# Group-norm statistics of a fused conv/scan kernel: sums and squares on ScalarE in place of block statistics on VectorE

## Chip, cores and metric

The kernel runs on one core of one Trainium2 chip. The metric is the device time of one execution in microseconds (us), lower is better; the time before is the median of three runs.

## What is computed

The input x has 16 images of 8 channels of 256 x 256, float32. Four residual blocks follow each other, and each normalises its input over four groups of two channels first (`_gn`):

```python
def _gn(v, G=4, eps=1e-05):
    g = v.reshape(B_, G, C_ // G, H_, W_)
    m = jnp.mean(g, axis=(2, 3, 4), keepdims=True)
    s = jnp.var(g, axis=(2, 3, 4), keepdims=True)
    return ((g - m) / jnp.sqrt(s + eps)).reshape(v.shape)

x = x + dilate3x3(_gn(x))                 # maximum over 3x3
x = x + mamba(_gn(x), ...)                # 4x4 pixel unshuffle: 128 channels, 4096 tokens, 256 inner rows, 32 states
x = x + conv3x3(_gn(x), L2_weight, L2_bias)
x = x + conv3x3(_gn(x), L3_weight, L3_bias)
```

The mamba block is a layer norm, an input projection with a causal convolution of 4 taps, SiLU, projections to dt, B and C, and for each of 32 states s the recurrence h = h * exp(dt * A_s) + (dt * x) * B_s over the 4096 tokens, y = sum over s of h * C_s, a gate and an output projection. A mean and a variance of each group of each image are what the change makes in another way; four such norms an image (called raw, x1, z0 and z1, after the tile that holds the input of each block).

## The kernel before

Everything is one program of five engine queues that are written by hand, with semaphores between them. A loop runs over the 16 images (b); in it stand 8 chunks of 512 tokens (c), and in each chunk the 32 states (s). One step (c, s) is called a state or slot here, (0, 14) for state 14 of chunk 0. Each engine's queue is written state by state, and all other work (the next chunk's projections, the dilation of the next image, the convolutions of the image before) is placed by tables into states of the queue: an engine does, at the end of what a state needs, what the tables put there.

In each state:
- ScalarE (ACT): `make_decay` makes exp(dt * A) of the *next* state in two halves into the PSUM ring `a_ps`, which has three places. Each half waits for the scan that last read its place. Then `keep` copies two columns (`carry`).
- VectorE (DVE): `scan` runs the recurrence for two halves of 128 rows x 512 tokens, out of `a_ps` and `u_in` into `h`; between them `make_u` multiplies `u_in` for the next state, out of `dtx` and `b_ps`. That is so in 22 of 32 states.
- GpSimd (POOL): `hc` = h * C of the state, and in the other 10 states `make_u`. `h` has three places, so VectorE can be at most some two states ahead of GpSimd. For each chunk GpSimd also multiplies one tile for the layer norm (`scale_tokens`, state 1), makes dt and dtx (states 23 to 27), and in chunks 1 to 4 adds the dilated rows (state 18).
- TensorE (PE): `b_ps` (the broadcast of B) for `make_u`, and the sum of `hc` over the states into `y_ps`.
- `gate` on VectorE at state 2 of a chunk waits until TensorE has summed the last state of the chunk before.

In certain states ScalarE also has the bursts that the argument comes back to: `silus` at state 14 of each chunk (two table loads and two activations), `split_hi` at 16, `softplus_in` at 21 and 23, `softplus_log` at 23, `centered` at 0, `token_rstd` at 2, `layer_norm` at 4, four `pad` (the normalised input of a convolution) a convolution, and `normalise_band` at state 6 of chunks 1 to 4.

The statistics before. VectorE reads each block of 512 elements once with the block statistics instruction (`partition_stats`, L1125), 8 blocks a norm: raw at (0, 9) to (0, 16), z0 at (0, 14) to (0, 21), z1 one by one after each block of the first convolution is copied out (in states 23, 29 and 3 of chunks 1 to 3), x1 at (5, 24) to (5, 30) and (6, 18). `group_local` (L1142) puts the 8 blocks together into a mean and a variance of each partition. TensorE then averages over the partitions of a group with a small matrix (L951), once for the mean (`group_mean`), and once for the variance plus the squared deviation of the partition's mean (`group_var`); ScalarE has `group_deviation` and `group_rstd` between and after. In chunk 0 VectorE waits for z to land before the first statistic of z0:

```python
if s == Z_STATS[1]:
    dve.wait_ge(z_in, (b + 1) * BANDS * 16)
last = z_stats(Z0, s - Z_STATS[1])
```

The blocks of z come by four DMAs that SyncE issues in states 9 to 12 of chunk 0, each of them behind a load of `c_sb` that waits for GpSimd's `hc` of that state or the one before.

Before the loop the norms of raw and x1 of the first image are made alone, behind their loads and with nothing beside them; behind the loop those of z0 and z1 of the last image.

## Time and profile before

| | |
|---|---|
| median of 3 runs | 14811.7 us (14810.26 to 14811.98) |
| profiled execution | 14813.43 us, its span 14811.6 us |
| TensorE busy | 12503.6 us, 84% |
| VectorE busy | 13954.9 us, 94% |
| ScalarE busy | 9028.1 us, 61% |
| GpSimd busy | 13564.0 us, 92% |
| granted TensorE clock, mean | 0.951 |
| idle time of GpSimd before `hc` | 839.6 us, of which 688.3 us ended by a scan of VectorE |

Busy time is the union of an engine's instructions. An instruction's duration overlaps that of its neighbour by some hundredths of a microsecond, so what an instruction adds to a queue without gaps is a little less than its duration. The loop over images lies between 217.27 us (the first `gate`) and 14637.67 us (the last), some 901 us an image. The stages below are cut at the start of `gate`, at state 2 of one chunk to state 2 of the next. Two engines are over 90% busy and hand each other work in every state, so a share of the span does not tell which one decides; that is read from who waits in which stretch.

How the views below read. The page and the groups by line give busy us, then (in groups) the mean ns of one, and behind the second bar the idle us just before them with what ended it. A window gives its length, then busy us and (x instructions) of TensorE, its weight loads, VectorE, ScalarE and GpSimd, the granted clock, the DMA share and GB/s. A timeline row has the start, the duration, engine, line and operation, the number merged (x), and in brackets the idle time before it.

### The profile page before, as it was taken

Reading aid. Unit: us, or ns where it says so; the run is one execution under the profiler, and the core shown is the slowest. Engines: PE = TensorE matmul, PEld = TensorE weight load, DVE = VectorE, ACT = ScalarE, POOL = GpSimd, SP = SyncE. Lnnn points to the kernel's source line nnn. Section 1 sums busy time; section 2 is a strip of 40 time slices with the busy share of each in tenths; the row PEclk is TensorE's granted clock in tenths of the full one; section 3 lists DMA queues with packets and bytes.
Section 4 is the critical chain, followed back from the end, with each engine's and each line's share of the span. In section 5 each row is a group of like instructions: output and inputs, shape, how many; then the busy total and the mean of one; then the engine's idle time right before and its main releaser. Section 6 shows DMA issues by size and latency. Waiting matters only on the chain.

```text
span 14811.6 us, 162715 instructions
## 1 busy us (share of the span) xinstructions
PE 12503.6 (84%) x27626; PEld 4938.6 (33%) x27626; DVE 13954.9 (94%) x12371; ACT 9028.1 (61%) x16239; POOL 13564.0 (92%) x6104
## 2 busy tenths in 40 slices
PE   4888878888888888888888888888888888888887
PEld 1333333333333333333333333333333333333332
DVE  5999999999999999999999999999999999999995
ACT  3666666666565666666666666665666666666663
POOL 4999999999999999999999999999999999999995
PEclk7999999999999999999999999999999999999998
DMA  3344443434434344443444434444343444434442
GB/s 92 108 121 115 115 121 108 127 111 114 121 110 128 108 115 122 114 122 109 116 121 115 120 109 123 114 115 121 110 129 107 114 123 114 122 110 115 121 114 80
DMA packets 1258543, 1701.83 MB, mean 115 GB/s; under 512 B 402220, under 2 KB 551156, under 8 KB 1257268
## 3 DMA queue, kind: packets, MB, share of 16 engines
q1 hardware_dynamic: 1257364, 1689.83, 40.7%
q14 instruction: 892, 7.31, 0.2%
q8 instruction: 287, 4.70, 0.1%
HBM read 1525.80 MB, written 124.13 MB: 111 GB/s over the span
## 4 chain that ended last, share of the span: by engine, by line
DVE 28%; PE 28%; issue 22%; POOL 14%; ACT 2%; DMA 2%; DVEq 1%; SPq 1%; POOLq 0%; ACTq 0%
PE y_ps L1026 17%; DVE h L1193 15%; POOL hc L659 10%; DVE u_in L1177 9%; PE proj_ps L980 3%; POOL u_in L636 3%; PE b_ps L1078 2%; PE side_ps L1037 2%; PE y_ps L1023 2%; DVE vmax L1156 1%; DMA z<-x_dram 1%; DVE stats L1125 1%; PE side_ps L1012 1%; DMA c_sb<-bc_dram 1%; DVEq L1191 1%
## 5 line engine op out<-in xcount | busy, mean ns | idle before, releaser
L659 POOL TENSOR_TENSOR hc<-h,c_sb 128x1024 f32<-128x1024 f32 x4096 | 9605.0, 2364 | 839.6 <-DVE h L1193 688.3
L1193 DVE TENSOR_TENSOR_SCAN h<-a_ps,carry,u_in 128x512 f32<-128x512 f32 x7168 | 8765.9, 1263 | 193.2 <-ACT a_ps L792 120.5
L792 ACT ACTIVATE a_ps<-dt,a_neg 128x512 f32<-128x512 f32 x8192 | 5602.5, 688 | 5166.5 <-DVE h L1193 5148.7
L1026 PE MATMUL y_ps<-hc,ident 128*128 128x512 f32 x16400 | 8169.3, 624 | 470.9 <-POOL hc L659 410.5
L1026 PEld LDWEIGHTS y_ps<-hc,ident 128*128 128x128 f32 x16400 | 3153.3, 198 | 4182.5 <-issue 3105.7
L1177 DVE TENSOR_TENSOR u_in<-dtx,b_ps 128x1024 f32<-128x1024 f32 x2816 | 3361.8, 1194 | 59.5 <-PE b_ps L1078 56.8
L636 POOL TENSOR_TENSOR u_in<-dtx,b_sb 128x1024 f32<-128x1024 f32 x1282 | 3033.8, 2367 | 0.1
L1078 PE MATMUL b_ps<-b_parts,select 96*128 96x512 bf16 x2816 | 1120.2, 398 | 1412.5 <-DVE u_in L1177 1410.4
L1193 DVE TENSOR_TENSOR_SCAN h<-a_ps,u_in 128x512 f32<-128x512 f32 x1024 | 1199.1, 1205 | 165.2 <-POOL hc L659 125.7
L1078 PEld LDWEIGHTS b_ps<-b_parts,select 96*128 96x128 bf16 x2816 | 281.9, 100 | 2944.9 <-DVE u_in L1177 2424.7
L980 PE MATMUL proj_ps<-u_ln,w_x 128*128 128x512 f32 x2064 | 974.2, 594 | 21.9 <-ACT xz L749 18.2
L1037 PE MATMUL side_ps<-padded,w_main 128*128 128x512 f32 x1632 | 872.1, 620 | 120.4 <-ACT raw L829 69.6
L798 ACT ACTIVATE carry<-h 128x2 f32<-128x2 f32 x3584 | 681.6, 190 | 0.0
L980 PEld LDWEIGHTS proj_ps<-u_ln,w_x 128*128 128x128 f32 x2064 | 390.9, 190 | 525.1 <-issue 489.3
L1041 PE MATMUL side_ps<-z,ident 128*128 128x512 f32 x544 | 517.4, 1040 | 0.0
L1037 PEld LDWEIGHTS side_ps<-padded,w_main 128*128 128x128 f32 x1632 | 320.8, 201 | 574.5 <-issue 414.6
L610 POOL TENSOR_TENSOR dt<-xz 128x512 f32<-128x512 f32 x258 | 329.5, 1277 | 61.6 <-ACT xz L783 61.6
L623 POOL TENSOR_TENSOR vmax<-norm,raw 128x1024 f32<-128x1024 f32 x68 | 277.0, 4074 | 94.3 <-DVE norm L1159 94.3
L1046 PE MATMUL side_ps<-edge,w_dt 49*128 49x512 f32 x544 | 333.8, 696 | 0.0
L617 POOL TENSOR_TENSOR dtx<-dt,xc 128x512 f32<-128x512 f32 x258 | 330.6, 1282 | 0.0
L801 ACT ACTIVATE padded<-z,g_shift,g_rstd 128x1024 f32<-128x1024 f32 x136 | 307.3, 2268 | 0.1
L1125 DVE BATCH_NORM_STATS2 stats<-z 128x6 f32<-128x512 f32 x272 | 180.6, 666 | 131.1 <-DMA z<-x_dram 69.0
(100 smaller groups left out, 6880.8 us busy)
## 6 DMA issues: line engine op xcount, KB each, us to landing
c_sb<-bc_dram SPq DMA_DIRECT2D x4100, 256.0 KB, 3.2
b_sb<-bc_dram SPq DMA_DIRECT2D x1284, 256.0 KB, 3.2
raw<-x SPq DMA_DIRECT2D x68, 512.0 KB
x_dram<-vmax SPq DMA_DIRECT2D x68, 512.0 KB, 4.7
z<-x_dram SPq DMA_DIRECT2D x68, 512.0 KB, 7.7
out<-raw SPq DMA_DIRECT2D x272, 128.0 KB
x_dram<-x SPq DMA_DIRECT2D x129, 256.0 KB, 3.9
x<-x_dram SPq DMA_DIRECT2D x136, 224.0 KB, 7.8
```

The costliest lines, as they stand in the source:

```text
L636: pool.tensor_tensor(u_in[:, s % U_RING], dtx[:, c % 2], b_sb[:, j % B_RING:j % B_RING + 1, :].broadcast_to([P, NH, T]), ALU.mult).then_in ...
L659: pool.tensor_tensor(hc[:, ring_at(c * S + s, HC_RING)], h[:, ring_at(c * S + s, H_RING)], c_sb[:, s // C_GROUP % C_RING, s % C_GROUP:s % ...
L792: act.activation(a_ps[:, a_slot(c * S + s, half)], dt[:, c % 2, half], ACT.Exp, scale=a_neg[:, at:at + 1]).then_inc(a_made, 1)
L798: act.activation(carry[:, :, s:s + 1], h[:, ring_at(c * S + s, H_RING), :, T - 1:T], ACT.Copy).then_inc(kept, 1)
L980: mm = pe.matmul(proj_ps[:, :], w_x[:, tap, half * P:(half + 1) * P], u_ln[:, tap:tap + T], start=(tap == 0), stop=(tap == TAPS - 1), skip ...
L1026: mm = pe.matmul(y_ps[:, half], ident[:, :], hc[:, ring_at((c * S + s) % (NC * S), HC_RING), half], start=False, stop=(s == S - 1), skip_g ...
L1037: pe.matmul(side_ps[:, :].rearrange("p (g w) -> p g w", w=W), w_main[n][:, part, :], padded[:, 1 + CB * k:1 + CB * (k + 1), part:part + W] ...
L1041: pe.matmul(side_ps[:, :].rearrange("p (g w q) -> p g w q", g=CB, q=R), ident[:, :], z[:, k * T:(k + 1) * T].rearrange("p (g q w) -> p g w ...
L1046: pe.matmul(side_ps[:, :], w_edge[n][:, :], edge[0:ER + 1, k % 2, :], start=False, stop=True, skip_group_check=True).then_inc(side_filled, 1)
L1078: pe.matmul(b_ps[:, :], select[:, k * P:(k + 1) * P], b_parts[:, c % 2, :], start=True, stop=True).then_inc(b_cast, 1)
L1177: dve.tensor_tensor(u_in[:, s % U_RING], dtx[:, c % 2], b_ps[:, :].unsqueeze(1).broadcast_to([P, NH, T]), ALU.mult).then_inc(u_made, 1)
L1193: dve.tensor_tensor_scan(h[:, r, half], a_ps[:, a_slot(c * S + s, half)], u_in[:, s % U_RING, half], start, ALU.mult, ALU.add).then_inc(h_ ...
```

## The change

VectorE loses all block statistics and `group_local`. ScalarE takes both passes:
- a first pass adds up each block: `sum_block` copies the block onto itself with the running sum of the instruction (`accum_out`) into `sums`; for z1 the sum rides on the copy out of PSUM that was there before (`copy_conv`).
- `group_mean` on TensorE takes 8 columns a norm in place of one; `group_average` on ScalarE adds the 8 columns and gives minus the group's mean.
- a second pass, `sum_squares`, reads each block again, as Square with the bias `g_mean`, with its running sum into `squares`, two blocks a state. What it writes goes into parts of `padded` or `norm` that are free then.
- `group_var` and `group_rstd` follow as before, with one more small activation and one more wait each.

The means move three states earlier (`MEAN_AT`), the variances 2 to 5 states later (`VAR_AT`), `pad` for z0 from (0, 28) to (1, 0) and for z1 from (4, 3) to (4, 5), the edge loads behind them, and block 6 of the second convolution from states 15 to 22 of chunk 6 to states 24 to 28.

```diff
-                            ((4, 0), (4, 1), (4, 2), (5, 0), (5, 1), (5, 2), (6, 0), (7, 0)))):
+                            ((4, 0), (4, 1), (4, 2), (5, 0), (5, 1), (5, 2), (6, 1), (7, 0)))):
     for k, (c, place) in enumerate(places):
         CONV_AT[n, k] = [c * S + s for s in PLACES[place]]
-MEAN_AT = {"joint": (0, 23), "z1": (3, 30), "x1": (6, 24)}
-VAR_AT = {"joint": (0, 26), "z1": (4, 1), "x1": (6, 27)}
+MEAN_AT = {"joint": (0, 20), "z1": (3, 30), "x1": (6, 21)}
+VAR_AT = {"joint": (0, 31), "z1": (4, 4), "x1": (6, 29)}
+SQUARES_AT = {"joint": [(0, s) for s in (21, 22, 24, 25, 26, 27, 28, 29)], "z1": [(3, 31), (4, 0), (4, 1), (4, 2)],
+              "x1": [(6, s) for s in (22, 24, 25, 26)]}
...
-PADDED_AT = ((0, 28), (4, 3))
-EDGES_AT = ((1, 0), (4, 8))
+PADDED_AT = ((1, 0), (4, 5))
+EDGES_AT = ((1, 5), (4, 10))
 LOAD_Z = (0, STORE_X2 + 1)
-RAW_STATS, Z_STATS = (0, 9), (0, 14)
-X1_STATS = [(5, 24 + k) for k in range(NC - 1)] + [(6, 18)]
+RAW_SUMS, Z_SUMS = (0, (9, 10, 11, 12)), (0, (14, 15, 16, 17))
+X1_SUMS = [(5, 24 + k) for k in range(NC - 1)] + [(6, 18)]
...
-                act.activation(g_mean[:, lo:hi], side_ps[:, 0:hi - lo], ACT.Copy, scale=-1.0).then_inc(side_emptied, 1)
+                group_average(g_mean, lo, hi, -1.0 / L).then_inc(side_emptied, 1)
                 act.wait_ge(side_emptied, read(b, "gn_mean", name))
+                act.sem_inc(gs, 1)
+            def group_average(dst, lo, hi, scale):
                 for n in range(lo, hi):
-                    made = act.activation(g_dev[:, n:n + 1], mv[:, n, 0:1], ACT.Square, bias=g_mean[:, n:n + 1])
-                made.then_inc(gs, 1)
-                act.wait_ge(gs, at + 2)
-                for n in range(lo, hi):
-                    made = act.activation(g_var[:, n:n + 1], g_dev[:, n:n + 1], ACT.Identity, bias=mv[:, n, 1:2])
-                made.then_inc(gs, 1)
+                    last = act.activation(few[:, int(scale > 0), n, :], side_ps[:, (n - lo) * NC:(n - lo + 1) * NC], ACT.Copy,
+                                          scale=scale, accum_out=dst[:, n:n + 1])
+                return last
+            def add_up(kind, k, src):
+                return act.activation(src, src, ACT.Copy, accum_out=sums[:, kind, k:k + 1])
+            def block_of(kind, k):
+                if kind == RAW:
+                    return raw[:, 1 + 2 * k:3 + 2 * k, :].rearrange("p a w -> p (a w)")
+                return (x1 if kind == X1 else z)[:, k * T:(k + 1) * T]
+            def sum_block(b, name, kind, k):
+                last = add_up(kind, k, block_of(kind, k))
+                if k == NC - 1 and kind == NORMS[name][1] - 1:
+                    last.then_inc(gs, 1)
+            def sum_squares(b, name, n):
+                lo, hi = NORMS[name]
+                kind, k = lo + n // (NC // 2), n % (NC // 2)
+                if n == 0:
+                    act.wait_ge(gs, norm_number(b, name) * GS + 2)
+                for k in (2 * k, 2 * k + 1):
+                    at = k if kind == X1 else (kind - lo) * NC + k
+                    places = 3 if kind == X1 else NC
+                    unused = (norm[:, 2 * (at % 3):2 * (at % 3) + 2, 1:W + 1] if kind == X1 else
+                              padded[:, 1 + CB * k:1 + CB * (k + 1), 1:W + 1])
+                    if at >= places:
+                        act.wait_ge(squared, squares_before(b, name) + at - places + 1)
+                    last = act.activation(unused, block_of(kind, k).rearrange("p (a w) -> p a w", w=W), ACT.Square,
+                                          bias=g_mean[:, kind:kind + 1],
+                                          accum_out=squares[:, kind, k:k + 1]).then_inc(squared, 1)
+                if n == (hi - lo) * NC // 2 - 1:
+                    act.wait_ge(squared, squares_before(b, name) + (hi - lo) * NC)
+                    act.sem_inc(gs, 1)
...
-                act.activation(g_log[:, lo:hi], side_ps[:, 0:hi - lo], ACT.Ln, bias=eps_col[:, :]).then_inc(side_emptied, 1)
+                group_average(g_var, lo, hi, 1.0 / L).then_inc(side_emptied, 1)
                 act.wait_ge(side_emptied, read(b, "gn_var", name))
+                act.activation(g_log[:, lo:hi], g_var[:, lo:hi], ACT.Ln, bias=eps_col[:, :]).then_inc(g_logs, 1)
+                act.wait_ge(g_logs, norm_number(b, name) + 1)
                 act.activation(g_rstd[:, lo:hi], g_log[:, lo:hi], ACT.Exp, scale=-0.5).then_inc(ga, 1)
...
+            def whole_norm(b, name, summed=0):
+                lo, hi = NORMS[name]
+                if not summed:
+                    for k in range(NC):
+                        sum_block(b, name, lo, k)
+                group_deviation(b, name)
+                for n in range(NC // 2):
+                    sum_squares(b, name, n)
+                group_rstd(b, name)
...
-                act.activation(block_o if n else block_z, side_ps[:, :].rearrange("p (g w q) -> p g q w", g=CB, q=R),
-                               ACT.Copy).then_inc(side_emptied, 1)
+                src = side_ps[:, :].rearrange("p (g w q) -> p g q w", g=CB, q=R)
+                if n:
+                    act.activation(block_o, src, ACT.Copy).then_inc(side_emptied, 1)
+                else:
+                    act.activation(block_z, src, ACT.Copy, accum_out=sums[:, Z1, k:k + 1]).then_inc(side_emptied, 1)
+                    if k == NC - 1:
+                        act.wait_ge(side_emptied, read(b, *use))
+                        act.sem_inc(gs, 1)
...
-            group_deviation(0, "raw_first")
-            group_rstd(0, "raw_first")
+            act.wait_ge(raw_in, RAW_DMAS * 16)
+            whole_norm(0, "raw_first")
             halo_scales(0)
             for k in range(BANDS):
                 normalise_band(0, k)
-            group_deviation(0, "x1_first")
-            group_rstd(0, "x1_first")
+            act.wait_ge(x1_in, X1_DMAS * 16)
+            whole_norm(0, "x1_first")
...
+                        if c == RAW_SUMS[0] and s in RAW_SUMS[1]:
+                            if s == RAW_SUMS[1][0]:
+                                act.wait_ge(raw_in, (b + 2) * RAW_DMAS * 16)
+                            for k in range(2):
+                                sum_block(b, "joint", RAW, 2 * RAW_SUMS[1].index(s) + k)
+                        if c == Z_SUMS[0] and s in Z_SUMS[1]:
+                            if s == Z_SUMS[1][0]:
+                                act.wait_ge(z_in, (b + 1) * BANDS * 16)
+                            for k in range(2):
+                                sum_block(b, "joint", Z0, 2 * Z_SUMS[1].index(s) + k)
+                        if (c, s) in X1_SUMS:
+                            k = X1_SUMS.index((c, s))
+                            if k in (0, NC - 1):
+                                act.wait_ge(x1_in, (b + 1) * X1_DMAS * 16 + (k // (NC - 1) + 1) * C * 16)
+                            sum_block(b, "x1", X1, k)
                         for name in VAR_AT:
                             if MEAN_AT[name] == (c, s):
                                 group_deviation(b, name)
+                            if (c, s) in SQUARES_AT[name]:
+                                sum_squares(b, name, SQUARES_AT[name].index((c, s)))
                             if VAR_AT[name] == (c, s):
...
+            act.wait_ge(z_in, (B + 1) * BANDS * 16)
             for n, name in enumerate(("z0_last", "z1_last")):
-                group_deviation(B, name)
-                group_rstd(B, name)
+                whole_norm(B, name, n)
...
-                    mm = pe.matmul(side_ps[:, n - lo:n - lo + 1], (group_z if n in (Z0, Z1) else group_m)[:, :],
-                                   rhs(n), start=True, stop=True, skip_group_check=True)
+                    mm = pe.matmul(side_ps[:, (n - lo) * NC:(n - lo + 1) * NC],
+                                   (group_z if n in (Z0, Z1) else group_m)[:, :],
+                                   rhs[:, n, :], start=True, stop=True, skip_group_check=True)
                 mm.then_inc(side_filled, 1)
 
             def group_mean(b, name):
                 pe.wait_ge(gs, norm_number(b, name) * GS + 1)
                 take_scratch(b, "gn_mean", name)
-                group_product(b, name, lambda n: mv[:, n, 0:1])
+                group_product(b, name, sums)
 
             def group_var(b, name):
                 pe.wait_ge(gs, norm_number(b, name) * GS + 3)
                 take_scratch(b, "gn_var", name)
-                group_product(b, name, lambda n: g_var[:, n:n + 1])
+                group_product(b, name, squares)
...
-            def partition_stats(kind, k, src):
-                return dve.bn_stats(stats[:, kind, k, :], src)
-            def raw_stats(k):
-                return partition_stats(RAW, k, raw[:, 1 + 2 * k:3 + 2 * k, :].rearrange("p a w -> p (a w)"))
-            def z_stats(kind, k):
-                return partition_stats(kind, k, z[:, k * T:(k + 1) * T])
-            def x1_stats(k):
-                return partition_stats(X1, k, x1[:, k * T:(k + 1) * T])
-            def group_local(b, name):
-                lo, hi = NORMS[name]
-                dve.wait_ge(st, norm_number(b, name) + 1)
-                dve.memset(spare[:, :], 0.0)
-                for n in range(lo, hi):
-                    last = dve.bn_aggr(mv[:, n, :], stats[:, n, :, :])
-                last.then_inc(gs, 1)
...
-                        if c == RAW_STATS[0] and 0 <= s - RAW_STATS[1] < NC:
-                            if s == RAW_STATS[1]:
-                                dve.wait_ge(raw_in, (b + 2) * RAW_DMAS * 16)
-                            raw_stats(s - RAW_STATS[1])
-                        if c == Z_STATS[0] and 0 <= s - Z_STATS[1] < NC:
-                            if s == Z_STATS[1]:
-                                dve.wait_ge(z_in, (b + 1) * BANDS * 16)
-                            last = z_stats(Z0, s - Z_STATS[1])
-                            if s - Z_STATS[1] == NC - 1:
-                                last.then_inc(st, 1)
-                                group_local(b, "joint")
-                        if (c, s) in X1_STATS:
-                            k = X1_STATS.index((c, s))
-                            if k in (0, NC - 1):
-                                dve.wait_ge(x1_in, (b + 1) * X1_DMAS * 16 + (k // (NC - 1) + 1) * C * 16)
-                            last = x1_stats(k)
-                            if k == NC - 1:
-                                last.then_inc(st, 1)
-                                group_local(b, "x1")
```

VectorE's queue, states 15 and 16 of chunk 0, in the kernel before: `h` is a scan (two in a row where GpSimd makes the next `u_in`), `stats` a block statistic.

```order
L1193 SCALAR_TENSOR_TENSOR h<-a_ps,u_in 128x512
L1174 REGISTER_ALU
L1177 TENSOR_TENSOR u_in<-dtx,b_ps 128x1024
L1193 SCALAR_TENSOR_TENSOR h<-a_ps,u_in 128x512
L1125 BN_STATS stats<-raw 128x6
L1125 BN_STATS stats<-z 128x6
L1186 REGISTER_ALU
L1191 ISA
L1193 SCALAR_TENSOR_TENSOR h<-a_ps,u_in 128x512 x2
L1125 BN_STATS stats<-raw 128x6
L1125 BN_STATS stats<-z 128x6
```

The same states in the changed kernel:

```order
L1248 SCALAR_TENSOR_TENSOR h<-a_ps,u_in 128x512
L1229 REGISTER_ALU
L1232 TENSOR_TENSOR u_in<-dtx,b_ps 128x1024
L1248 SCALAR_TENSOR_TENSOR h<-a_ps,u_in 128x512
L1241 REGISTER_ALU
L1246 ISA
L1248 SCALAR_TENSOR_TENSOR h<-a_ps,u_in 128x512 x2
```

Two statistics a state are gone from VectorE, with z's wait in the state before; the scans stand as they did.

ScalarE's queue in the kernel before from `silus` in state 14 to state 15 of chunk 0 (`a_ps` is a half of the next state's decay, `xc` and `zs` are the two SiLUs, `carry` is `keep`):

```order
L758 ACTIVATE xc<-xz 128x1024
L759 ACTIVATE zs<-xz 128x1024
L760 ACT_TABLE_LOAD
L790 REGISTER_ALU
L792 ACTIVATE a_ps<-dt,a_neg 128x512
L790 REGISTER_ALU
L792 ACTIVATE a_ps<-dt,a_neg 128x512
L797 ISA
L798 ACTIVATE carry<-h 128x2
```

The same place in the changed kernel:

```order
L818 ACTIVATE xc<-xz 128x1024
L819 ACTIVATE zs<-xz 128x1024
L820 ACT_TABLE_LOAD
L979 ISA
L705 ACTIVATE z,sums<-z 128x512 x2
L850 REGISTER_ALU
L852 ACTIVATE a_ps<-dt,a_neg 128x512
L850 REGISTER_ALU
L852 ACTIVATE a_ps<-dt,a_neg 128x512
L857 ISA
L858 ACTIVATE carry<-h 128x2
L705 ACTIVATE z,sums<-z 128x512 x2
```

The wait for z (L979) and two sums now stand between the second table load and the decay of state 16, and two more sums follow that decay. In states 16 and 17 two sums stand behind the splits in the same way.

## Rows read from the trace of the kernel before

**Rows 1.** the page, busy us (share) xinstructions of each engine

```profile
PE 12503.6 (84%) x27626; PEld 4938.6 (33%) x27626; DVE 13954.9 (94%) x12371; ACT 9028.1 (61%) x16239; POOL 13564.0 (92%) x6104
```

**Rows 2.** windows, four chunks of one image, sum of all eight

```profile
4728.12:4846.64 118.52, 87.71 (x200) 34.72 (x200) 109.92 (x110) 76.26 (x141) 105.23 (x48) 0.94 0.48 131
...
5188.16:5302.61 114.45, 100.00 (x223) 39.20 (x222) 110.23 (x94) 76.31 (x130) 106.17 (x48) 0.97 0.39 108
5302.61:5411.03 108.42, 98.30 (x223) 39.26 (x222) 106.85 (x96) 68.93 (x128) 105.30 (x49) 0.98 0.54 128
5411.03:5518.26 107.23, 90.25 (x207) 36.31 (x206) 104.01 (x92) 68.39 (x130) 101.81 (x47) 0.97 0.38 110
...
sum 901.05, PE 765.35 PEld 303.49 DVE 867.97 ACT 559.63 POOL 845.06; mean PE 95.67 PEld 37.94 DVE 108.50 ACT 69.95 POOL 105.63
```

**Rows 3.** groups by line, VectorE's block statistics, whole span

```profile
L1125 DVE BATCH_NORM_STATS2 stats<-z 128x6 f32<-128x512 f32 x272 | 180.6, 666 | 131.1 <-DMA z<-x_dram 69.0 <-ACT z L829 62.1
...
L1125 DVE BATCH_NORM_STATS2 stats<-raw 128x6 f32<-128x512 f32 x136 | 90.4, 669 | 27.0 <-DMA raw<-x 27.0
```

**Rows 4.** groups by line, VectorE, chunk 0, from z's landing on

```profile
L1193 DVE TENSOR_TENSOR_SCAN h<-a_ps,u_in 128x512 f32<-128x512 f32 x15 | 17.8, 1198 | 0.0
L1177 DVE TENSOR_TENSOR u_in<-dtx,b_ps 128x1024 f32<-128x1024 f32 x5 | 5.9, 1187 | 0.0
L1125 DVE BATCH_NORM_STATS2 stats<-z 128x6 f32<-128x512 f32 x8 | 5.4, 670 | 2.7 <-DMA z<-x_dram 2.7
L1125 DVE BATCH_NORM_STATS2 stats<-raw 128x6 f32<-128x512 f32 x2 | 1.3, 668 | 0.0
...
L1142 DVE BATCH_NORM_AGGREGATE mv<-stats 128x2 f32<-128x48 f32 x2 | 0.6, 340 | 0.0
```

**Rows 5.** groups by line, GpSimd, the same stretch

```profile
L659 POOL TENSOR_TENSOR hc<-h,c_sb 128x1024 f32<-128x1024 f32 x9 | 21.1, 2354 | 11.0 <-DVE h L1193 11.0
...
L610 POOL TENSOR_TENSOR dt<-xz 128x512 f32<-128x512 f32 x1 | 1.3, 1264 | 0.6 <-ACT xz L783 0.6
```

**Rows 6.** timeline at z's landing, VectorE, then ScalarE

```profile
4776.33 0.69 DVE L1125 BATCH_NORM_STATS2 stats<-z 128x6 f32<-128x512 f32 x1 [2.66 <-DMA z<-x_dram]
...
4771.71 1.28 ACT L758 ACT_TABLE_LOAD   x1
...
4775.03 1.28 ACT L760 ACT_TABLE_LOAD   x1
4776.32 0.69 ACT L792 ACTIVATE a_ps<-dt,a_neg 128x512 f32<-128x512 f32 x1
```

**Rows 7.** groups by line, ScalarE activations near the new ones

```profile
L792 ACT ACTIVATE a_ps<-dt,a_neg 128x512 f32<-128x512 f32 x8192 | 5602.5, 688 | 5166.5 <-DVE h L1193 5148.7 <-issue 3.1 <-POOL dt L610 2.0
...
L734 ACT ACTIVATE xz<-xz 128x512 f32<-128x512 f32 x129 | 81.3, 630 | 4.1
...
L819 ACT ACTIVATE x<-side_ps 128x512 f32<-128x512 f32 x129 | 76.8, 595 | 105.3 <-PE side_ps L1015 105.3
...
L739 ACT ACTIVATE u_ln<-u_ln 128x3 f32<-128x3 f32 x112 | 21.0, 188 | 0.0
```

**Rows 8.** timeline, GpSimd, end of chunk 0, chunk 1 and chunk 6

```profile
4842.22 6.96 POOL L659 TENSOR_TENSOR hc<-h,c_sb 128x1024 f32<-128x1024 f32 x3
...
4876.81 2.36 POOL L659 TENSOR_TENSOR hc<-h,c_sb 128x1024 f32<-128x1024 f32 x1 [0.94 <-DVE h L1193]
...
5469.44 2.35 POOL L659 TENSOR_TENSOR hc<-h,c_sb 128x1024 f32<-128x1024 f32 x1 [1.45 <-DVE h L1193]
```

**Rows 9.** timeline, VectorE in chunk 4 behind the four pads

```profile
5209.41 3.65 DVE L1193 TENSOR_TENSOR_SCAN h<-a_ps,carry,u_in 128x512 f32<-128x512 f32 x3 [1.43 <-ACT a_ps L792]
```

**Rows 10.** timeline, VectorE, first raw norm and last z0 norm

```profile
60.87 4.84 DVE L1125 BATCH_NORM_STATS2 stats<-raw 128x6 f32<-128x512 f32 x8 [26.95 <-DMA raw<-x]
...
14657.10 4.84 DVE L1125 BATCH_NORM_STATS2 stats<-z 128x6 f32<-128x512 f32 x8 [18.20 <-DMA z<-x_dram]
```

**Rows 11.** waits, TensorE on VectorE's statistics: us, times, longest

```profile
PE side_ps L951 <- DVE mv L1142: 186.0, 20, 86.3
```

45 lines of the change are left out of this document (11 added, 34 removed).

## The prediction

> **What bounds the kernel now.** I read the page first: VectorE is busy for 94% of the span and GpSimd for 92%, ScalarE for 61% [rows 1]. A share does not choose between two engines that feed each other, so the next view is busy time by chunk. Over one image VectorE works 868.0 us and GpSimd 845.1 us of 901.1 us, ScalarE 559.6 us [rows 2]. The reader should take two things from this. ScalarE has some 341 us an image to spare. And VectorE could lose only 23 us an image before GpSimd, whose work the change does not touch, has more to do than VectorE; each of them already idles 33 and 56 us an image, since `h` has three places and neither can run far from the other.
>
> So what a removed instruction is worth depends on whether GpSimd waits for VectorE soon behind it. The timeline of GpSimd shows a pattern in each chunk. From dt on (state 23) it works without a gap over the chunk's end and on to state 9 of the next one: three `hc` in a row end the chunk, and its first wait for VectorE in chunk 1 is 0.94 us at 4876.81 [rows 8]. In states 10 to 22 it waits for VectorE every few states. Work taken from VectorE in the first part only lengthens its lead, which `gate` takes away again at state 2, since it waits for the last `hc` and its sum on TensorE. Work taken in the second part shortens the chunk. Chunk 5 checks this: it holds seven statistics of x1 in states 24 to 30, some 4.2 us of VectorE, and yet is only 1.2 us longer than chunk 6 (108.42 against 107.23) [rows 2].
>
> Chunk 0 is the place that matters. It takes 118.5 us with GpSimd busy for 105.2 [rows 2]. VectorE waits 2.66 us for z at 4776.33 [rows 6] and then has ten statistics and two aggregations in eight states [rows 4]. From z's landing to the first dt, GpSimd idles 11.0 us before nine `hc`, all ended by VectorE, and 0.6 us for ScalarE's softplus [rows 5].
>
> **Prices.** Eight block statistics in a row take 4.84 us, 0.6 us each [rows 10]; their mean is 666 to 669 ns with the overlap [rows 3]. An aggregation is 0.34 us [rows 4]. Per image 32 statistics and 4 aggregations leave VectorE: 32 x 0.6 + 4 x 0.34 = 20.6 us.
>
> On ScalarE no activation here writes a running sum, so I bound it. Without it, a copy of 512 columns out of PSUM is 595 ns and an activation in SBUF with constants 630 ns; one with a scale from a column of SBUF is 688 ns [rows 7]. A sum block is nearest to 630, a square block (bias from a column) to 688; in a run some 0.07 us of each overlaps. The running sum costs between nothing and a whole extra instruction of the shortest kind, 188 ns [rows 7]; between them I take 0.1, since about half of a short instruction disappears under its neighbours in the timeline. So 0.65 us a sum block and 0.7 us a square block. Per image: 24 x 0.65 + 32 x 0.7 + 8 x 0.1 (the sums that ride on z1's copies) + some 2 us of small ones = 41 us, an eighth of ScalarE's idle time.
>
> A rule bears on this price. The Trainium skill (VectorE: DVE Perf Modes, Two Vector instructions with no wait between them) says that an op which also writes out its accumulator is two instructions, the second a read of the accumulator. It says so of VectorE only, and no run here shows it yet for ScalarE. Were it so there too, my 0.1 would be that second instruction; at its full 188 ns the 41 us would be 47.
>
> **The change, part by part, per image.**
>
> Chunk 0, up to state 13: five raw statistics leave VectorE. Nothing is gained, since GpSimd has no gap there, and z's last DMA is issued only when GpSimd has done its `hc` of state 11; z lands when it did.
>
> Chunk 0, z's landing to dt. ScalarE's second table load ends at 4776.31 [rows 6], the moment z lands, so its new wait for z costs little. The decay of state 15 is made before it. Before: z lands, one statistic (0.6), state 15 (two scans and one `u_in` of mean 1.20 and 1.19 us, 3.4 net [rows 4]), two statistics (1.2): state 16 starts 5.2 us after z. After: state 15 is done while z is awaited, and state 16 waits for two sums and one half decay on ScalarE, 1.3 + 0.7: 2.0 us after z. That gains 3.2. Behind it VectorE has 7 statistics and 2 aggregations less, 4.9 us. But ScalarE has states 15 to 17 full: each has two decays and `keep` (1.3) and two sums (1.3), and state 16 three split copies of 0.57 net (1.7, as the copy of [rows 7]): 9.5 us, against 8.6 on VectorE for the three states of scans that they feed (3.4 where it makes `u_in`, 2.3 in the two where GpSimd does, 0.6 for `split_rest`). That is 0.9 late, and I add 1.1 for states 21 to 23, where the squares meet `softplus_in` and `softplus_log`: 2.0 off. Sum: -3.2 - 4.9 + 2.0 = **-6.1**, out of the 11.6 that GpSimd idles. From dt on GpSimd is full: up to its last `hc` seven others and three `u_in` of about the same length (10 x 2.35) and two dt and two dtx (4 x 1.26) [rows 5], 28.5 us for eight states. ScalarE then has two decays, `keep` and two squares a state, 2.7 us against 3.5: covered. If that cover were gone, each 0.1 us over 3.5 would cost 0.6 us in the six states.
>
> `pad` in states (1, 0) to (1, 3), beside `centered` and `token_rstd`: ScalarE falls behind by some 4 us there, VectorE's lead covers it, 0.
>
> Statistics of z1: six stand in states 23 and 29, covered by GpSimd, 0. Two stand in state 3 of chunks 2 and 3, behind `gate`, where VectorE starts its next lead: 2 x 0.6 = **-1.2**. TensorE waited for the aggregation at z1's mean (part of 186.0 us in 20 waits, most of it at the first image [rows 11]); that stall goes, and I give it **-0.5**.
>
> Chunk 4: before, the pads made VectorE wait 1.43 us at state 8 [rows 9]. Two states later and with `group_rstd` in front, they meet `copy_x` and `residual` of state 7: I put **+0.8** on it.
>
> Statistics of x1: the seven in chunk 5 are covered, **-0.3** for the little that shows. The eighth, at (6, 18), with its aggregation, stands right before GpSimd's wait of 1.45 us [rows 8]: 0.6 + 0.4 = **-1.0**.
>
> Sum: -6.1 - 1.2 - 0.5 + 0.8 - 0.3 - 1.0 = -8.3 us an image, x 16 = **-133 us**. This is two fifths of the 330 us taken from VectorE.
>
> Outside the loop nothing runs beside the norms. Raw, x1 and the last z0: 8 statistics and an aggregation (5.2 us) and two small activations give way to 8 sums (5.2) and 8 squares (5.6) on ScalarE, +5.6 each; the last z1 has its sums with the copies and gains 8 squares, +4.8. Together **+22 us**.
>
> The profiled execution took 14813.4 us, 1.7 over the median; the sum against it is 14813.4 - 133 + 22 = 14702. Against the median I say **14700 us**, 0.75% faster.
>
> **The rivals.** A measurement of this kernel can tell 0.2%, some 30 us, from no change.
>
> *VectorE bounds everywhere.* For it: VectorE has the least idle time in nearly every window. Against it: chunk 5 beside chunk 6. Then all 20.6 x 16 = 330 us count: 14813 - 330 + 22 = 14505. Chance 0.12.
>
> *Only the wait moves.* ScalarE is held by z longer than VectorE was, and GpSimd and TensorE absorb most of the rest: chunk 0 gives 4 in place of 6.1, chunk 3 and 6 nothing more than 0.5: 14813 - 16 x 4 + 22 = 14771. For it: z has DMAs that land later in some images. Chance 0.15.
>
> *ScalarE becomes the bound in chunk 0, and the kernel gets slower.* Its place is states 14 to 17 and 21 to 29. If the running sum costs e more than my 0.1 us an instruction, eight of them lie before state 18 (8e), four before softplus (4e), and in the six states of 24 to 29 two each, free until a state is over 3.5 us, which is at e = 0.4. At e = 0.4: 8e + 4e = 4.8, about 1 more in chunks 4 and 6, and 56 instructions outside the loop, 22 us: 14813 - 16 x 2.5 + 44 = 14817, no change. From there it decides: at e = 0.6 it is 7.2 + 2.4 + 1.5 = 11.1 against 8.3, +45, and +56 outside: 14914. The Trainium skill (ScalarE: Activation LUTs, Rules for kernel authors) speaks for this one: it wants sums and products on VectorE, not ScalarE. Against it stands the idle time of ScalarE and its most expensive near row, 688 ns. Chance 0.08 for slower, 0.07 for about equal.
>
> *The forecast*, between 14640 and 14760: chance 0.58.
>
> **How the numbers follow.** Faster by over 0.2% (under 14782): the forecast, VectorE everywhere, and four fifths of the moved wait: 0.58 + 0.12 + 0.12 = 0.82. Within 0.2%: 0.03 + 0.07 = 0.10. Slower: 0.08. The range leaves out the full 330 us case and the slower one: 14580 (a running sum that costs nothing, and half of the covered statistics counting after all: -8.3 - 0.8 - 5 = -14 an image, 14611, and a little beyond) to 14795.
>
> **What would show it right or wrong.** In the changed profile: no statistics on VectorE; ScalarE at about 65%; its sum blocks at some 0.65 to 0.75 us and squares 0.7 to 0.8, anything near 1 us speaks for the slower rival. Chunk 0 at about 112 us and GpSimd's idle time between z and dt down to 5 or 6 us; chunks 1 and 7 as before; chunk 5 at 108. VectorE waits for ScalarE in states 16 to 19 of chunk 0. If chunk 5 falls by 3 or 4 us, VectorE bound everywhere. The forecast fails if z's wait on ScalarE grows past what VectorE had, or if `gate` comes later because TensorE, not GpSimd, ends the chunk.

## The result and the profile after

The changed kernel takes 14720.7 us (median of 4 runs, 14718.2 to 14730.5) against 14811.0 us (4 runs). The ratio is 0.9940, with a 95% interval of 0.9928 to 0.9952: 90 us or 0.6% faster. The forecast was 14700 us, in a range from 14580 to 14795.

The page of the changed kernel, the line that answers to [rows 1]:

```profile
PE 12490.3 (85%) x27626; PEld 4914.0 (33%) x27626; DVE 13645.9 (93%) x11707; ACT 9618.0 (65%) x18363; POOL 13562.3 (92%) x6104
```

VectorE has lost 309 us of busy time and ScalarE gained 590, and yet the span is only 93 us shorter. GpSimd, whose work the change does not touch, tells where to look: its idle time before `hc` has fallen from 839.6 us to 725.4, by 114 us, which is what the loop over images has lost (below). Groups by line:

```profile
L662 POOL TENSOR_TENSOR hc<-h,c_sb 128x1024 f32<-128x1024 f32 x4096 | 9597.7, 2363 | 725.4 <-DVE h L1248 543.1 <-PE y_ps L1110 122.0 <-DMA c_sb<-bc_dram 58.6
```

Windows say where the 93 us are. These are chunks 0, 4, 5 and 6 of the same image as in [rows 2], and the last row is that whole image:

```profile
4703.23:4817.32 114.09, 89.78 (x200) 35.21 (x200) 100.50 (x91) 91.76 (x207) 106.39 (x49) 0.94 0.49 136
5156.46:5272.12 115.66, 99.49 (x225) 39.12 (x224) 110.34 (x94) 79.08 (x141) 107.77 (x49) 0.99 0.37 108
5272.12:5379.92 107.80, 100.03 (x223) 39.59 (x222) 103.36 (x90) 72.65 (x141) 103.49 (x48) 0.97 0.57 127
5379.92:5486.16 106.24, 90.13 (x207) 35.43 (x206) 103.05 (x89) 74.49 (x151) 103.45 (x48) 0.98 0.39 113
4703.23:5597.02 893.79, 764.24 (x1713) 301.44 (x1712) 850.17 (x730) 594.15 (x1133) 844.53 (x381) 0.97 0.42 118
```

Chunk 0 is shorter, chunk 4 is longer by 1.2 us, and chunk 5, which lost 3.5 us of VectorE, by 0.6 only. One image is not enough, since chunks 0, 3, 5, 6 and 7 vary by 1 to 5 us from image to image. The means over the 16 images, from `gate` to `gate` in both traces, are: chunk 0 from 119.3 to 112.6 (-6.7), chunk 1 113.1 (0), chunk 2 -0.4, chunk 3 0, chunk 4 from 114.4 to 115.7 (+1.2), chunk 5 -0.4, chunk 6 -1.0, chunk 7 +0.1. That is -7.2 an image, -115 us. The rest is outside the loop: the first `gate` starts at 227.43 in place of 217.27 us, and from the last one to the end it is 185.3 in place of 174.0 us: +21.5 us.

In chunk 0, the timeline of ScalarE and VectorE at z's landing, which answers to [rows 6]:

```profile
4747.63 1.28 ACT L820 ACT_TABLE_LOAD   x1
...
4752.77 0.63 ACT L705 ACTIVATE z<-z 128x512 f32<-128x512 f32 x1 [3.86 <-DMA z<-x_dram]
4753.31 0.19 ACT L705 ACTIVATION_READ_ACCUMULATOR z<-z 128x1 f32 x1
4753.40 0.61 ACT L705 ACTIVATE z<-z 128x512 f32<-128x512 f32 x1
...
4754.01 1.28 ACT L852 ACTIVATE a_ps<-dt,a_neg 128x512 f32<-128x512 f32 x2
...
4754.71 2.34 DVE L1248 TENSOR_TENSOR_SCAN h<-a_ps,u_in 128x512 f32<-128x512 f32 x2 [5.67 <-ACT a_ps L852]
```

In this image ScalarE waits 3.86 us for z, with the decay of state 16 queued behind, and VectorE waits 5.67 us for that decay. It is one of the longer waits: over the 16 images of the loop ScalarE waits 38.0 us for z, 2.4 an image, where VectorE had waited 50.8, or 3.2 an image (totals of 52.7 and 69.0 us, less the one wait behind the loop, 14.7 and 18.2). State 16 starts 1.9 us after z has landed; before, it was 5.2. GpSimd in the stretch from z's landing to the first dt, by line, answers to [rows 5]:

```profile
L662 POOL TENSOR_TENSOR hc<-h,c_sb 128x1024 f32<-128x1024 f32 x9 | 21.1, 2357 | 6.3 <-DVE h L1248 6.3
```

and the dt behind it in the timeline:

```profile
4783.54 1.27 POOL L613 TENSOR_TENSOR dt<-xz 128x512 f32<-128x512 f32 x1 [0.39 <-ACT xz L843]
```

11.6 us of idle time have become 6.7. The new instructions of ScalarE, by line over the whole span (they answer to [rows 3] and [rows 7]):

```profile
L732 ACT ACTIVATE padded<-z,g_mean 128x512 f32<-128x512 f32 x272 | 192.5, 710 | 0.2
...
L705 ACT ACTIVATE z<-z 128x512 f32<-128x512 f32 x136 | 83.6, 615 | 52.7 <-DMA z<-x_dram 52.7
...
L732 ACT ACTIVATION_READ_ACCUMULATOR padded<-z,g_mean 128x1 f32 x272 | 51.2, 188 | 0.0
```

A square is 0.71 us, a sum 0.61, and each running sum is a second instruction of 0.19 us. What they add to the queue is read where nothing else runs. Timeline of ScalarE at the first raw norm, in place of [rows 10]:

```profile
60.75 0.63 ACT L705 ACTIVATE raw<-raw 128x512 f32<-128x512 f32 x1 [29.39 <-DMA raw<-x]
61.29 0.19 ACT L705 ACTIVATION_READ_ACCUMULATOR raw<-raw 128x1 f32 x1
61.38 0.61 ACT L705 ACTIVATE raw<-raw 128x512 f32<-128x512 f32 x1
...
69.66 0.71 ACT L732 ACTIVATE padded<-raw,g_mean 128x512 f32<-128x512 f32 x1
70.27 0.19 ACT L732 ACTIVATION_READ_ACCUMULATOR padded<-raw,g_mean 128x1 f32 x1
70.37 0.71 ACT L732 ACTIVATE padded<-raw,g_mean 128x512 f32<-128x512 f32 x1
```

From one start to the next it is some 0.61 us for a sum and 0.70 for a square. The read starts under the activation's tail and ends under the next one's head: 0.09 us of the pace lie between its start and the next activation's.

### The profile page after: what moved, and what is told of

It reads as the page before. It is cut to its first block, busy times and chain, and to the rows that moved or that the text cites. A ratio compares the mean times of both kernels' runs of the same rounds, so it can differ in the third digit from the quotient of the medians.

```text
span 14718.6 us, 164375 instructions
## 1 busy us (share of the span) xinstructions
PE 12490.3 (85%) x27626; PEld 4914.0 (33%) x27626; DVE 13645.9 (93%) x11707; ACT 9618.0 (65%) x18363; POOL 13562.3 (92%) x6104
## 4 chain that ended last, share of the span: by engine, by line
PE 29%; DVE 23%; issue 22%; POOL 15%; ACT 5%; DMA 3%; SPq 1%; DVEq 1%; POOLq 1%; ACTq 0%
PE y_ps L1110 17%; DVE h L1248 12%; POOL hc L662 12%; DVE u_in L1232 8%; PE proj_ps L1064 3%; POOL u_in L639 2%; PE side_ps L1121 2%; PE b_ps L1162 2%; DMA c_sb<-bc_dram 2%; DVE vmax L1219 1%; ACT a_ps L852 1%; PE y_ps L1107 1%; PE side_ps L1096 1%; DMA z<-x_dram 1%; PE side_ps L1099 1%
## 5 line engine op out<-in xcount | busy, mean ns | idle before, releaser
L662 POOL TENSOR_TENSOR hc<-h,c_sb 128x1024 f32<-128x1024 f32 x4096 | 9597.7, 2363 | 725.4 <-DVE h L1248 543.1
L1110 PEld LDWEIGHTS y_ps<-hc,ident 128*128 128x128 f32 x16400 | 3118.6, 196 | 4393.1 <-issue 3066.3
L1219 DVE TENSOR_REDUCE vmax<-norm 128x516 f32<-128x1548 f32 x136 | 258.8, 1903 | 65.2 <-ACT norm L871 43.6
```

The lines of the kernel that those rows point to most:

```text
L662: pool.tensor_tensor(hc[:, ring_at(c * S + s, HC_RING)], h[:, ring_at(c * S + s, H_RING)], c_sb[:, s // C_GROUP % C_RING, s % C_GROUP:s % ...
L1110: mm = pe.matmul(y_ps[:, half], ident[:, :], hc[:, ring_at((c * S + s) % (NC * S), HC_RING), half], start=False, stop=(s == S - 1), skip_g ...
L1219: ins = dve.tensor_reduce(vmax[:, row:row + R // 2, :], rows_of_3, mybir.AxisListType.X, ALU.max)
```

## The experiments

Each kernel was timed beside the kernel before, whose median was 14811.6 us with the first four, 14813.6 with the next four (from joint_left_out on) and 14813.9 with the last four; differences to it are taken within their group. Chunk means are over the 16 images of its trace; the first two rows are for comparison.

| kernel | median us | ratio to before, 95% | c0 | c3 | c4 | c5 | c6 |
|---|---|---|---|---|---|---|---|
| before | 14811.0 | | 119.3 | 114.0 | 114.4 | 108.6 | 107.9 |
| the change | 14720.7 | 0.9940 (0.9928 to 0.9952) | 112.6 | 114.0 | 115.7 | 108.2 | 106.9 |
| joint_only | 14708.4 | 0.9928 (0.9915 to 0.9942) | 112.8 | 114.1 | 114.4 | 108.5 | 107.5 |
| z1_x1_only | 14808.5 | 0.9998 (0.9989 to 1.0007) | 120.0 | 114.0 | 115.9 | 108.1 | 107.1 |
| joint_x1 | 14689.3 | 0.9916 (0.9903 to 0.9930) | 112.8 | 114.4 | 114.4 | 107.8 | 106.8 |
| joint_x1_late | 14634.6 | 0.9880 (0.9865 to 0.9895) | 109.7 | 113.9 | 114.4 | 107.9 | 106.9 |
| joint_left_out | 14743.1 | 0.9951 (0.9937 to 0.9965) | 114.8 | 114.2 | 114.4 | 108.5 | 107.5 |
| z1_x1_left_out | 14788.7 | 0.9982 (0.9973 to 0.9991) | 119.7 | 113.2 | 114.4 | 107.1 | 108.5 |
| z_a_state_later | 14775.2 | 0.9975 (0.9965 to 0.9984) | 117.6 | 113.9 | 114.4 | 108.6 | 107.8 |
| z1_timetable | 14837.3 | 1.0014 (1.0005 to 1.0023) | 120.5 | 114.4 | 115.6 | 108.1 | 107.4 |
| change_z_sums_later | 14668.7 | 0.9902 (0.9887 to 0.9917) | 110.0 | 113.6 | 115.7 | 107.7 | 107.3 |
| late_by_one | 14641.8 | 0.9880 (0.9865 to 0.9895) | 110.5 | 113.8 | 114.4 | 107.8 | 106.7 |
| late_by_three | 14608.1 | 0.9857 (0.9842 to 0.9872) | 108.5 | 113.6 | 114.4 | 108.2 | 107.2 |
| one_square_more | 14745.8 | 0.9950 (0.9936 to 0.9964) | 113.9 | 113.8 | 115.8 | 107.8 | 107.0 |

Chunks 1, 2 and 7 are at 113.0 to 113.1, 113.1 to 113.4 and 110.6 to 110.8 in all of them, but for chunk 1 of the last (113.7). Chunk 2 has two values, 113.1 in the five kernels that take z1's statistics from VectorE and 113.4 in all others. Chunk 0 differs by up to 1.2 us between traces of kernels that are alike there (119.3, 119.7, 120.0, 120.5), chunk 3 by 0.8 and chunks 5 and 6 by about half a microsecond, so the medians decide and the chunks say where. Chunk 4 differs by less than 0.1 from image to image in most of them.

### The change taken apart

Which norms go by ScalarE became a table in one kernel with both ways in it; the timetable of each norm goes with its way.

```diff
+BY_SCALAR = ("joint",)             # joint_only
+BY_SCALAR = ("z1", "x1")           # z1_x1_only
+BY_SCALAR = ("joint", "x1")        # joint_x1
+                if name not in BY_SCALAR:
...
+                        if "joint" not in BY_SCALAR and c == RAW_STATS[0] and 0 <= s - RAW_STATS[1] < NC:
```

**joint_only.** 

> Of the change only the part on the joint norm (raw and z0 in chunk 0, with its timetable) is made; z1, x1 and the norms outside the loop keep VectorE's block statistics. Coupling theory (a removed instruction counts only where GpSimd soon waits for VectorE): nearly the whole gain of the full change sits here, and neither the loss in chunk 4 nor the 22 us outside the loop: chunk 0 shorter by 6.7 us as in the full change, x 16 = -107, so about 14704 us, a little below the full change (14721). Rival, VectorE bounds everywhere: 16 statistics and two aggregations at 0.6 and 0.34 us are 10.3 us an image, -165, 14646. Rival, ScalarE's bursts already eat part of it: the joint norm alone gives less than 100 us.

It took 103 us off, against 107 expected. Chunk 0 gives all of it (6.45 x 16 = 103).

**z1_x1_only.** 

> Of the change only the parts on z1 and x1 inside the loop, with their timetable; the joint norm and those outside the loop keep the block statistics. 16 statistics and two aggregations leave VectorE here too, as many as in the run of the joint norm alone. Coupling theory, from the changes by chunk of the full change (-0.3, +1.3, -0.4, -1.0): -0.4 us an image, -6 us, so 14805, the same as before within 0.2%. Rival, VectorE bounds everywhere: 10.3 us an image as for the joint norm, 14646.

3 us faster, with an interval that holds zero. The same number of VectorE's instructions is gone as in joint_only, and their price on VectorE is the same. This run also has the new timetable of z1, which costs some 24 us by itself (z1_timetable below); even with these given back it is far from the 165 us of the rival in which VectorE bounds everywhere. Where the work stood is what counted.

**joint_x1.** 

> Joint norm and x1 inside the loop on ScalarE; z1 (with its old timetable) and all norms outside the loop on VectorE. Coupling theory: -6.7 in chunk 0, -0.4 in chunk 5, -1.0 in chunk 6, no loss in chunk 4, x 16 = -130: 14681, some 40 us under the full change, half of it from chunk 4 (1.3 x 16 = 21) and half from outside the loop (22). Rival, the gain of x1 was only given from one chunk to the next: same as the joint norm alone, 14704.

14689, 8 us over the expectation and 31 under the full change, from which it differs in chunk 4 and outside the loop. x1 gives 19 us over joint_only. Its own timetable came with it and has no run: in z1_timetable, where x1's statistics stay on VectorE, chunks 5 and 6 are at 108.1 and 107.4 already.

### VectorE's side alone

```diff
# joint_left_out
-                            raw_stats(s - RAW_STATS[1])
+                            if s - RAW_STATS[1] == NC - 1:
+                                raw_stats(s - RAW_STATS[1])
...
-                            last = z_stats(Z0, s - Z_STATS[1])
                             if s - Z_STATS[1] == NC - 1:
+                                last = z_stats(Z0, s - Z_STATS[1])
# z1_x1_left_out: the same condition for x1_stats(k) and conv_stats(...)
# z_a_state_later
-RAW_STATS, Z_STATS = (0, 9), (0, 14)
+RAW_STATS, Z_STATS = (0, 9), (0, 15)
```

**joint_left_out.** 

> The kernel before, with 14 of the 16 block statistics of the joint norm (raw and z0, blocks 0 to 6) left out inside the loop and nothing put in their place, so raw and z0 are normalised with wrong constants; timetable, waits, aggregations as before. It prices VectorE's side of chunk 0 alone. Coupling theory: the five raw statistics before z are worth nothing, the nine behind z 0.6 us each: -5.4 us an image, -86, about 14725. Rival, VectorE bounds everywhere: 14 x 0.6 = 8.4, -134, 14677. Rival, only the wait for z matters: it stays here, so no more than 20 us.

It took 70 us off, 4.4 us an image: 16 less than the coupling theory said, and half of what the 14 instructions had on VectorE. Groups by line, VectorE; the statistics of z and the wait for z now stand before the scan that has no `carry`, that of chunk 0:

```profile
L1194 DVE TENSOR_TENSOR_SCAN h<-a_ps,u_in 128x512 f32<-128x512 f32 x1024 | 1191.2, 1205 | 267.0 <-POOL hc L659 125.5 <-DMA z<-x_dram 87.9 <-ACT a_ps L792 27.0
...
L1126 DVE BATCH_NORM_STATS2 stats<-z 128x6 f32<-128x512 f32 x160 | 105.4, 662 | 81.2 <-ACT z L829 63.2 <-DMA z<-x_dram 18.0
```

The waits for z have grown from 69.0 us [rows 3] to 87.9 + 18.0: the last is the wait behind the loop (18.2 before), so inside the loop it is 87.9 in place of 50.8. These 37 us are three quarters of what the five raw statistics before z's landing took (5 x 0.6 x 16 = 48): most of that work has become waiting time.

**z1_x1_left_out.** 

> The kernel before, with the block statistics 0 to 6 of z1 and of x1 left out inside the loop, 14 again, so z1 and x1 are normalised with wrong constants. Coupling theory: two in state 3 were forecast at 0.6 each and measured at 0.3 together, the others are covered by GpSimd: -0.3 to -1.5 us an image, 14787 to 14806. VectorE bounds everywhere: 8.4 us, 14677, as for the joint norm. It also tells whether the 0.3 was small because ScalarE took the work (then more here) or because VectorE's lead in state 3 is worth nothing (then the same).

25 us by the medians, 27 by the ratio, against 134 for the rival. It is the pair to joint_left_out: 14 statistics gone from VectorE and nothing put in their place, 25 us here and 70 there. Chunk 3 falls to 113.2; the four kernels with z1 on ScalarE have 113.6 to 114.0, the nine with its statistics on VectorE 113.6 to 114.4. So VectorE's statistics in state 3 were worth something, and work placed on ScalarE in the change seems to give most of it back. Seven statistics in chunk 5 give 1.4, of which chunk 6 returns 0.6.

**z_a_state_later.** 

> The kernel before with one number changed: the statistics of z0 stand in states 15 to 22 in place of 14 to 21. No work is taken from VectorE; its 2.66 us wait for z goes, since z lands while it works on state 15. If only the wait matters: all of 2.7 us counts, -43, 14768. If VectorE's work behind z is what bounds and the wait is part of it, the same -43; that the wait is worth nothing (the statistics behind are as late) gives 14811. The full change's chunk 0 gain of 6.7 us then splits into this part and that of the work taken away.

38 us faster for one number. The same group as above:

```profile
L1125 DVE BATCH_NORM_STATS2 stats<-z 128x6 f32<-128x512 f32 x272 | 180.3, 665 | 79.3 <-ACT z L829 60.2 <-DMA z<-x_dram 19.0
```

The waits for z fall by 50 us, from 69.0 to 19.0 (one of those left, 18.2 us, is behind the loop, [rows 10]), and three quarters of that show in the time. That is a part of the gain that needs no work moved. It does not simply add to the 70 us of joint_left_out, where the wait stayed and had grown.

### Chunk 4

```diff
-MEAN_AT = {"joint": (0, 23), "z1": (3, 30), "x1": (6, 24)}
-VAR_AT = {"joint": (0, 26), "z1": (4, 1), "x1": (6, 27)}
+MEAN_AT = {"joint": (0, 23), "z1": (3, 30), "x1": (6, 21)}
+VAR_AT = {"joint": (0, 26), "z1": (4, 4), "x1": (6, 29)}
...
-PADDED_AT = ((0, 28), (4, 3))
-EDGES_AT = ((1, 0), (4, 8))
+PADDED_AT = ((0, 28), (4, 5))
+EDGES_AT = ((1, 0), (4, 10))
```

**z1_timetable.** 

> The kernel before, with only the timetable of the change for z1 and x1: the rstd of z1 at (4, 4) in place of (4, 1), its pads at (4, 5) in place of (4, 3), its edge loads at (4, 10), block 6 of the second convolution 9 states later, the mean and rstd of x1 at (6, 21) and (6, 29). The statistics stay on VectorE and no squares are made. If the 1.3 us that chunk 4 lost come from the pads' place, beside copies and residual of state 7: +13 to +21 us, 14825 to 14832. If they come from the squares and the reads of the accumulators in states 0 to 2 on ScalarE: the same as before, 14811.

24 us slower, interval 7 to 34, near the expected 13 to 21. The window of chunk 4 of the image of [rows 2] (there 114.45):

```profile
5190.35:5306.02 115.67, 103.42 (x225) 40.61 (x224) 110.12 (x95) 77.84 (x135) 107.84 (x49) 0.94 0.35 108
```

Chunk 4 has its loss in full (115.6 in the mean) with no square on ScalarE, so the timetable costs it. The trace says which part. TensorE's output projection (L1012), by line, in the kernel before and then here:

```profile
L1012 PE MATMUL side_ps<-zs,w_out 128*128 128x512 f32 x516 | 242.6, 592 | 1.3 <-DVE zs L1208 1.3
```

```profile
L1012 PE MATMUL side_ps<-zs,w_out 128*128 128x512 f32 x516 | 244.2, 596 | 30.9 <-ACT g_log L704 29.6 <-DVE zs L1208 1.3
```

and the timeline at states 4 to 6 of this chunk:

```profile
5200.25 0.24 ACT L704 ACTIVATE g_log<-side_ps,eps_col 128x1 f32<-128x1 f32 x1
5200.54 1.98 PE L1012 MATMUL side_ps<-zs,w_out 128*128 128x512 f32 x4 [1.85 <-ACT g_log L704]
...
5205.80 0.38 PE L1078 MATMUL b_ps<-b_parts,select 96*128 96x512 bf16 x1
...
5206.22 1.22 DVE L1177 TENSOR_TENSOR u_in<-dtx,b_ps 128x1024 f32<-128x1024 f32 x1 [1.83 <-PE b_ps L1078]
```

The variance of z1 is in the PSUM tile `side_ps`, which the projection needs next. With the rstd at (4, 4) ScalarE reads it later, TensorE stands 1.85 us, in every image (16 x 1.85 = 29.6), `b_ps` for the next `u_in` comes late behind it, and VectorE waits 1.83 us. The trace of the change has the same two waits, 1.86 and 1.84 us. The wait of [rows 9] for a decay behind the pads, 1.43 us, is down to 0.60 in this run and 0.62 in the change: the rstd costs chunk 4 its time, not the pads. A run with the rstd alone moved was not made. Chunk 4 is 19 of the 24 us. Chunk 0, where nothing was edited, is 1.2 us longer too and chunks 5 and 6 half a microsecond shorter each, within the differences named above.

### The place of z's sums, and the cover of the squares

```diff
-RAW_SUMS, Z_SUMS = (0, (9, 10, 11, 12)), (0, (14, 15, 16, 17))
+RAW_SUMS, Z_SUMS = (0, (9, 10, 11, 12)), (0, (16, 17, 18, 19))   # change_z_sums_later, joint_x1_late
+RAW_SUMS, Z_SUMS = (0, (9, 10, 11, 12)), (0, (15, 16, 17, 18))   # late_by_one
+RAW_SUMS, Z_SUMS = (0, (9, 10, 11, 12)), (0, (17, 18, 19, 20))   # late_by_three, mean at (0, 21)
```

**joint_x1_late.** 

> As the run of joint and x1, with the sums of z0 two states later, (0, 16) to (0, 19) in place of (0, 14) to (0, 17). In the full change ScalarE waited 4.3 us for z at state 14, and the scan of state 16 then waited 5.7 us for its decay. Theory that this wait still costs: it disappears, since z lands while VectorE works on state 15, and up to 3 of GpSimd's remaining 6.3 us of idle time behind z go: 14681 - 16 x 2 to 3 = 14635 to 14650. Rival, the wait costs nothing because the sums are as late behind it: 14681 again, or a few us more, since state 19 and the mean at state 20 now follow directly.

14634.6: 55 us less than joint_x1, the edge of the expected range. (The expectation gives ScalarE's wait for z as 4.3 us; in the traced image it is 3.86.)

**change_z_sums_later.** 

> The changed kernel with one edit: the sums of z0 at (0, 16) to (0, 19) in place of (0, 14) to (0, 17). The wait of the scan of state 16 for its decay (5.7 us in the traced image) goes. Theory that ScalarE held by z's landing starves VectorE and with it GpSimd: the same 3.4 us an image as in the run of joint and x1 (14689 to 14635), so 14721 - 55 = 14666. Rival, that gain had come from other places of that mixed kernel: less than 20 us.

52 us less than the change. The scans of chunk 0, by line, in the change and then with the sums later:

```profile
L1248 DVE TENSOR_TENSOR_SCAN h<-a_ps,u_in 128x512 f32<-128x512 f32 x1024 | 1199.6, 1207 | 257.3 <-POOL hc L662 146.5 <-ACT a_ps L852 88.4 <-POOL u_in L639 16.7
```

```profile
L1248 DVE TENSOR_TENSOR_SCAN h<-a_ps,u_in 128x512 f32<-128x512 f32 x1024 | 1197.6, 1208 | 187.1 <-POOL hc L662 140.6 <-ACT a_ps L852 23.7 <-POOL u_in L639 16.7
```

and ScalarE's wait for z in the latter:

```profile
L705 ACT ACTIVATE z<-z 128x512 f32<-128x512 f32 x136 | 83.3, 612 | 14.7 <-DMA z<-x_dram 14.7
```

ScalarE's wait for z was 52.7 us in the change and is 14.7, all of it behind the loop; VectorE's waits for a decay in chunk 0 fall from 88.4 to 23.7 us (before: 22.4).

**late_by_one.** 

> As joint and x1 with late sums, but one state later only: (0, 15) to (0, 18). z has landed by state 15, so if the wait alone was the cost, this is as fast as two states later, 14635. If what matters is that ScalarE's two table loads and SiLUs of state 14 are followed directly by other long work (sums at 15, copies of split_hi and sums at 16), half of the gain is lost: 14650 to 14665.

14641.8, 7 us over two states later, with the same ratio: leaving state 14 is nearly all of these 55 us. The expectation that z has landed by then does not hold, though. ScalarE still waits 19.8 us for it, 1.2 an image, but the decay of state 16 is now queued ahead of the wait:

```profile
4716.48 1.30 ACT L887 ACTIVATE a_ps<-dt,a_neg 128x512 f32<-128x512 f32 x2
...
4719.57 0.63 ACT L737 ACTIVATE z<-z 128x512 f32<-128x512 f32 x1 [1.67 <-DMA z<-x_dram]
```

The wait is half as long as in the change (38.0 us in the loop) and nearly all of its cost is gone; that fits a cost that comes from what is queued behind it.

**late_by_three.** 

> As joint and x1 with late sums, three states later: (0, 17) to (0, 20), the mean at state 21. State 16 with its three copies is free of sums. GpSimd now idles only 2.2 us behind z in the traced image, so at most 2 us an image are left; theory of coupling: 14620 to 14640. Rival, the mean and the first squares now come straight behind the last sum, ScalarE waits there for TensorE beside softplus_in: 14640 to 14660.

14608.1, 12 us under the expected range and the fastest of all: 1.4% under the kernel before and, by the two ratios, 0.8% under the change. Against late_by_one, on the same chip, it is 34 us less. Its chunk 0 of the same image, and GpSimd's only wait for VectorE behind z's landing there:

```profile
4661.80:4769.84 108.04, 88.79 (x200) 36.09 (x200) 100.53 (x91) 90.65 (x205) 105.01 (x48) 0.94 0.52 143
```

```profile
4724.81 2.35 POOL L683 TENSOR_TENSOR hc<-h,c_sb 128x1024 f32<-128x1024 f32 x1 [0.86 <-DVE h L1313]
```

Sums and the three copies of `split_hi` no longer share state 16. That this, and not the later mean, is what helped has no run of its own.

**one_square_more.**

```diff
+                if name == "joint":
+                    act.activation(nowhere[:, :], block_of(kind, k), ACT.Square, bias=g_mean[:, kind:kind + 1],
+                                   accum_out=spare_sum[:, 0:1]).then_inc(again, 1)
```

> The changed kernel with one more square block on ScalarE in each of the eight states of chunk 0 that make squares (21, 22, 24 to 29), its result unused. It prices the cover of which the forecast said that the squares beside GpSimd's full stretch cost nothing as long as a state of ScalarE stays under 3.5 us: it goes from 2.7 to 3.4. Cover theory: states 24 to 29 free, states 21 and 22 up to 0.7 each: 0 to +22 us, 14721 to 14743. Rival, ScalarE bounds chunk 0: all 8 x 0.7 = 5.6 us count, +90, 14811.

25 us slower than the change by the medians, just over the upper end of the cover theory, or 15 by the two ratios, inside it; both are far from 90. Timeline of ScalarE, from one pair of decays to the next:

```profile
4796.31 1.28 ACT L862 ACTIVATE a_ps<-dt,a_neg 128x512 f32<-128x512 f32 x2
4797.53 0.19 ACT L868 ACTIVATE carry<-h 128x2 f32<-128x2 f32 x1
4797.62 0.71 ACT L735 ACTIVATE padded<-z,g_mean 128x512 f32<-128x512 f32 x1
4798.24 0.19 ACT L735 ACTIVATION_READ_ACCUMULATOR padded<-z,g_mean 128x1 f32 x1
4798.33 0.71 ACT L735 ACTIVATE padded<-z,g_mean 128x512 f32<-128x512 f32 x1
...
4799.03 0.71 ACT L741 ACTIVATE nowhere<-z,g_mean 128x512 bf16<-128x512 f32 x1
...
4799.74 1.28 ACT L862 ACTIVATE a_ps<-dt,a_neg 128x512 f32<-128x512 f32 x2
```

A state of ScalarE is 3.43 us, where it was 2.73, and still under the 3.5 of the cover. Of 5.6 us added an image, 1.6 show (the medians give 25 / 16 = 1.6): 1.3 in chunk 0 and 0.6 in chunk 1, less what the others vary by. The cover is nearly used up: VectorE's waits for a decay in chunk 0 are 127.9 us in this run, 88.4 in the change.

## Why the prediction was right, and where its terms were off

**Which engine decides where.** Right. ScalarE came to 65%, chunk 0 to 112.6 for 112, chunk 5 to 108.2 for 108. z1_x1_only and joint_only take the same work from VectorE and give 3 and 103 us; with nothing put on ScalarE and the timetable kept it is 25 and 70 (the two left_out runs). The shares of the page, 94% and 92% [rows 1], would have priced them alike.

**Chunk 0, -6.1 an image.** Measured -6.7, but what was to be gained and what was taken off were both put too small, and that these errors nearly cancel is luck. The forecast took 3.2 for the wait and 4.9 for the work behind it, and 2.0 off for ScalarE's full states. On VectorE's side the work alone gives 4.4 us an image (joint_left_out) with 87.9 / 16 = 5.5 us of waiting for z still in it; of such a wait three quarters showed in z_a_state_later, so an estimate for both is 8.5. With the sums out of ScalarE's way, chunk 0 goes down to 108.5 (late_by_three), 10.8 under the kernel before. So at least 10.8 was to be had in place of 8.1, and the place of the sums in the change cost some 4 us an image in place of 2.0. The joint norm's new timetable (its pads at (1, 0) in place of (0, 28)) is in the 10.8 and not in the 8.5; it has no run of its own.

The start of state 16, 2.0 us after z, was forecast to a tenth of a microsecond (1.9). The sentence that ScalarE's new wait for z costs little is the step that failed. It was read from a table load that ended as z landed, 48.2 us behind the `gate` [rows 6]. In the same image of the change the load ends at 4748.91, 45.7 us behind the `gate`, since with five raw statistics fewer VectorE and ScalarE reach state 14 earlier, and z does not: it is there 48.2 us behind the `gate` in the mean of the 16 images, where it was 48.5. The prediction's own sign of failure, that z's wait on ScalarE grows past what VectorE had, is met in this image (3.86 against 2.66 us) and not over the loop (38.0 against 50.8). But behind this shorter wait stood decays: VectorE's waits for them rose from 22.4 to 88.4 us, by 4.1 an image.

**Raw statistics before z, 0.** Right in the main: in joint_left_out three quarters of them turn into waits for z.

**z1 in state 3, -1.2, and TensorE's wait, -0.5.** Wrong in the sum: chunks 2 and 3 gave 0.4. z1_x1_left_out gives 0.4 + 0.8 there, so the term for VectorE was about right, and in the change the part of chunk 3 is missing. That the mean and squares of z1 from (3, 30) on gave it back fits, but was not tried; the forecast had priced them at nothing. No run shows the -0.5 by itself.

**Chunk 4, +0.8.** Measured +1.2, and z1_timetable shows all of it without any square. That the timetable costs it was right, the mechanism (pads that meet `copy_x` and `residual` of state 7) was not: the wait behind the pads got shorter, 0.62 us for 1.43, and the loss is TensorE's wait for `group_rstd` at `side_ps`, 1.86 us, behind which VectorE waits 1.84 us for `b_ps`. That the number came near is luck.

**x1, -0.3 and -1.0.** Measured -0.4 and -1.0; joint_x1 less joint_only is 19 us, or 1.2 an image. How much of it is the new place of block 6 of the second convolution and of x1's mean is open. The cover of chunk 5 is not whole: with the seven statistics left out it is 1.4 us shorter.

**Outside the loop, +22.** Measured +21.5 from one trace to the other. Over the three traces with the change outside the loop and the eleven without it is 19, since the part behind the loop varies by 5 us. It needs nothing but the pace of the instructions, forecast at 0.65 us for a sum and 0.7 for a square, the running sum within: it is 0.61 and 0.70.

**The rivals.** VectorE everywhere fell with z1_x1_only and z1_x1_left_out. Only the wait moves: taking the wait alone away is worth 38 us, taking the statistics away and keeping the wait 70, so it fell too. ScalarE as the bound: the running sum stayed at some 0.1 us an instruction, as forecast, where this rival needed 0.4 on top of it, and with 5.6 us more an image the kernel is still faster than before. The rule of the Trainium skill that speaks for this one (ScalarE: Activation LUTs, Rules for kernel authors) lists `add` and `mul` for VectorE, not ScalarE, by the speed of one element. Which engine others wait for decided here: for the norm of chunk 0, where GpSimd waits for VectorE, the move to ScalarE gained 103 us, and for z1 and the norms outside the loop it gave nothing or a loss.

## What to carry to other kernels

Where two engines feed each other through a short ring, price a removed instruction by its place: it counts if the other engine waits soon behind it, and becomes waiting time if a transfer or a full partner comes next. When a wait moves to another engine's in-order queue, ask what is queued behind it and put it behind the transfer's landing; here four pairs of sums placed one state later were worth 47 us and three states later 81 (joint_x1 to late_by_one and late_by_three), nearly as much as the whole change. When a read of a shared PSUM tile is moved later, ask who fills that tile next: in chunk 4 this made VectorE wait 1.8 us an image, by way of TensorE, and the chunk 1.2 us longer. And a change made of parts that are independent should keep only those that pay: here the norm of chunk 0 and x1, not z1 and not the norms outside the loop.

## What the runs showed of the hardware that was not expected

A running sum on ScalarE is an instruction of its own in the trace, `ACTIVATION_READ_ACCUMULATOR`, with a duration of 186 to 194 ns, whatever the activation. Most of it lies under its neighbours: a square with it goes at a pace of 0.70 us, while the second of two decays, 512 columns with a scale from a column and no sum, starts some 0.61 us behind the first (two of them take 1.28 us). That is about 0.1 us for the running sum. The Trainium skill (VectorE: DVE Perf Modes, Two Vector instructions with no wait between them) states for VectorE that such an op is two instructions; this trace shows the same for ScalarE.

A square into a bf16 tile takes as long as one into f32, 0.71 us.
